# Recommendation tower on one core: loop over pairs of tiles, 14 tables selected on chip in place of 10, MLP on 256 columns

## What is computed

```python
e = jnp.stack([tbl_0[ids[:, 0]], ..., tbl_31[ids[:, 31]]], axis=1)   # 2048 x 32 x 128
dots = jnp.einsum('bfd,bgd->bfg', e, e)
z = dots[:, iu, ju]                                                 # the 496 pairs f < g
h = jnp.concatenate([z, dense_ctx], axis=1)                         # 2048 x 512
h = jnp.maximum(h @ W_top1 + b_top1, 0.0)                           # 512
h = jnp.maximum(h @ W_top2 + b_top2, 0.0)                           # 256
y = h @ W_top3                                                      # 1
```

## Time and profile before

| | |
|---|---|
| median of three runs | 483.03 us (482.62, 486.81, 483.03) |
| span of the profiled execution, first to last instruction | 482.2 us |
| mean granted TensorE clock | 0.915 of full |
| PE busy | 391.0 us, 81% |
| POOL busy | 335.4 us, 70% |
| DVE busy | 240.1 us, 50% |
| ACT busy | 150.2 us, 31% |
| busy share of the 16 DMA engines for gathers (q0), for SP's queue (q1) | 19.4%, 13.9% |
| moved | 41.81 MB |

### The profile page before, as it was taken

One profiled execution on the slowest core, in us unless ns is written; L12 is line 12 of the kernel. 1 busy time (PEld: TensorE's weight loads), 2 busy tenths in 40 slices (PEclk: granted clock), 3 DMA queues, 4 the chain that ended last, 5 costly groups with the idle time before them and its releaser, 6 DMA issues.

```text
span 482.2 us, 16007 instructions
## 1 busy us (share of the span) xinstructions
PE 391.0 (81%) x6624; PEld 362.7 (75%) x6624; DVE 240.1 (50%) x698; ACT 150.2 (31%) x315; POOL 335.4 (70%) x356
## 2 busy tenths in 40 slices
PE   0555669899989898968969898969879798967846
PEld 0554569797979797957969797959879697956836
DVE  1467479556555555635535655535645555411010
ACT  1032223242424243322404332413414232321411
POOL 5777707777777777777777777777777777777700
PEclk9857559899999999989979999989979999988988
DMA  6555843333333323233323333333323332222200
GB/s 139 157 170 175 222 118 89 90 74 91 79 89 76 91 72 90 74 81 79 81 70 83 80 82 86 76 89 77 77 67 87 75 89 63 56 57 53 56 9 0
DMA packets 30470, 41.81 MB, mean 87 GB/s; under 512 B 11986, under 2 KB 23010, under 8 KB 30404
## 3 DMA queue, kind: packets, MB, share of 16 engines
q0 software_dynamic: 11264, 23.09, 19.4%
q1 hardware_dynamic: 16804, 17.52, 13.9%
q10 hardware_dynamic: 2336, 0.19, 0.4%
HBM read 40.76 MB, written 0.01 MB: 85 GB/s over the span
## 4 chain that ended last, share of the span: by engine, by line
PE 59%; issue 12%; DMA 11%; POOL 9%; DVE 6%; ACT 2%; SPq 1%; POOLq 0%; DVEq 0%; ACTq 0%
PE sel_ps L279 26%; DMA rows_T<-tables_selected 11%; PE x_ps L311 10%; PE gram_ps L293 10%; POOL gathered L240 9%; PE rows_ps L264 6%; PE x_ps L320 5%; DVE onehot L500 3%; DVE pairs L508 2%; PE x_ps L327 1%; PE x_ps L302 1%; ACT table_hi L453 1%; DVE pairs L513 1%; DMA gathered<-table,tile_ids 1%; SPq L193 0%
## 5 line engine op out<-in xcount | busy, mean ns | idle before, releaser
L240 POOL DMA_INDIRECT gathered<-table,tile_ids x352 | 335.2, 952 | 122.2 <-issue 103.9
L500 DVE TENSOR_SCALAR onehot<-id_rows,row_no 128x256 fp32r<-128x256 int32 x640 | 198.8, 379 | 94.3 <-PE sel_ps L279 92.7
L279 PE MATMUL sel_ps<-onehot,table_hi 125*128 125x256 f32 x640 | 182.6, 317 | 38.2 <-DVE onehot L500 35.6
L279 PE MATMUL sel_ps<-onehot,table_lo 125*128 125x256 f32 x640 | 173.5, 302 | 2.1 <-issue 2.0
L279 PEld LDWEIGHTS sel_ps<-onehot,table_hi 125*128 125x128 f32 x640 | 134.8, 211 | 47.1 <-issue 43.1
L279 PEld LDWEIGHTS sel_ps<-onehot,table_lo 125*128 125x128 f32 x640 | 135.5, 212 | 0.6 <-issue 0.5
L399 ACT ACTIVATE rows_T<-sel_ps 128x256 f32<-128x256 f32 x80 | 50.4, 630 | 124.3 <-PE sel_ps L279 86.6
L293 PE MATMUL gram_ps<-rows_T 128*32 128x32 f32 x4096 | 57.7, 202 | 35.1 <-issue 31.6
L293 PEld LDWEIGHTS gram_ps<-rows_T 128*32 128x32 f32 x4096 | 47.8, 111 | 45.6 <-issue 41.0
L393 ACT ACTIVATE rows_T<-rows_ps 128x512 f32<-128x512 f32 x96 | 55.9, 589 | 68.8 <-PE rows_ps L264 64.9
L508 DVE STREAM_TRANSPOSE pairs<-gram_ps 128x1024 f32<-128x1024 f32 x16 | 20.0, 1250 | 97.5 <-PE gram_ps L293 97.5
(11 more groups left out here) (12 smaller groups left out, 47.4 us busy)
## 6 DMA issues: line engine op xcount, KB each, us to landing
id_rows<-ids_selected SPq DMA_DIRECT2D x80, 128.0 KB
gathered<-table,tile_ids POOLq DMA_INDIRECT x352
rows_T<-tables_selected SPq DMA_DIRECT2D x10, 500.0 KB
w_sb<-w SPq DMA_DIRECT2D x1, 1024.0 KB, 12.4
w_sb<-w SPq DMA_DIRECT2D x1, 512.0 KB, 14.1
tile_ids<-ids ACTq DMA_DIRECT2D x16, 11.0 KB
out<-y_sb ACTq DMA_DIRECT2D x16, 0.5 KB
mask<-upper_mask SPq DMA_DIRECT2D x1, 128.0 KB, 6.5
```

The source lines that it names most:

```text
L240: nc.gpsimd.indirect_dma_start(gathered[:, a % 2, g, :], None, tables_gathered[g], bass.IndirectOffsetOnAxis(ap=slot_id, axis=0)).then_inc ...
L279: last = nc.tensor.matmul(sel_ps[:, q % 2, 0, :], part[0:SEL_P, f, k, :], onehot[0:SEL_P, h, kk, :], start=(k == 0 and part is table_hi), ...
L500: last = nc.vector.tensor_scalar(onehot[:, h, kk, :], id_rows[:, slot, :], row_no[:, k:k + 1], None, ALU.is_equal)
```

## The change

- 14 tables are selected, 18 features gathered (chunks of 4, 4, 4, 4, 2 per tile, ten chunks in a pair).
- The unit of all loops is a pair of tiles. On PE, `selects(i, o)` holds 13 selections, the turns of chunks 0 to 7 and the network of the pair before; `grams(i, o)` holds the turns of chunks 8 and 9, the two `gram`, and between them the first selection of the next pair. PE, ACT and DVE loop over six pairs with one pair in the body, SP over seven. POOL's program is written out without a loop.
- `layer1`, `layer2`, `layer3` work on the 256 columns of a pair, except in the last pair, which goes through the network tile by tile behind its two `gram`.
- `rows_T` holds two tiles in place of four; a pair's first selection is copied into it after both `gram` of the pair before.
- Tables are loaded into four slots that lie in `pairs`, `x0` and `x1`, each as two transfers, of 112 and of 13 rows. Mask, dense values and weights come behind the last table. Eight of the first pair's ten chunks are turned between the selections of the start.
- All rows of `tile_ids` are loaded at the start, the first tile's by itself.

```diff
-N_SEL = 10
+N_SEL = 14
 SEL_ROWS = 1000
 SEL_K = 8
 SEL_P = SEL_ROWS // SEL_K
+SEL_P16 = SEL_P // 16 * 16
 K_HALF = SEL_K // 2
 N_GATH = N_FEAT - N_SEL
 CHUNK = 4
 CHUNKS = [(c, min(CHUNK, N_GATH - c)) for c in range(0, N_GATH, CHUNK)]
 NC = len(CHUNKS)
-SEL_PER_TILE = N_SEL // 2
 PAIR = 2 * P
-ROW_SLOTS = 4
-RAW_SLOTS = 8
+ROW_SLOTS = 5
+RAW_SLOTS = 4
...
-        rows_T = sb("rows_T", [P, 4, P, N_FEAT])
+        rows_T = sb("rows_T", [P, 2, P, N_FEAT])
...
+        raw_slots = [pairs[:, 0, :, :].rearrange("p g f -> p (g f)"),
+                     pairs[:, 1, :, :].rearrange("p g f -> p (g f)"),
+                     x0[:, :, :].rearrange("p k s -> p (k s)"),
+                     x1[:, :, :].rearrange("p k s -> p (k s)")]
...
+            def load_table(f):
+                if f >= RAW_SLOTS:
+                    sp.wait_ge(table_ready, f - RAW_SLOTS + 1)
+                sp.dma_start(raw(f)[0:SEL_P16, :], tables_selected[f, 0:SEL_P16, :]).then_inc(table_in[f], 16)
+                sp.dma_start(raw(f)[SEL_P16:SEL_P, :], tables_selected[f, SEL_P16:SEL_P, :]
+                             ).then_inc(table_in[f], 16)
+            load_table(0)
             sp.dma_start(row_no[:, :], row_numbers).then_inc(row_no_in, 16)
-            sp.dma_start(raw(0), tables_selected[0]).then_inc(table_in[0], 16)
             load_id_row(0, 0, 0)
+            load_table(1)
...
+            for p in range(n_pairs):
+                for t in range(2):
+                    if p == 0 and t == 0:
+                        pool.wait_ge(first_ids_in, 16)
+                    elif p == 0:
+                        pool.wait_ge(tile_ids_in, 16)
+                    for c, (first, n) in enumerate(CHUNKS):
+                        if p > 0:
+                            pool.wait_ge(chunk_turned, 2 * NC * (p - 1) + NC * t + c + 1)
+                        pool.nop(nofuse=True)
+                        for g in range(first, first + n):
+                            slot_id = tile_ids[:, 2 * p + t, g:g + 1]
+                            nc.gpsimd.indirect_dma_start(
+                                gathered[:, t, g, :], None, tables_gathered[g],
+                                bass.IndirectOffsetOnAxis(ap=slot_id, axis=0)).then_inc(chunk_in[t][c], 16)
...
+            def layer1(i, o, n):
+                if n == 0:
+                    pe.wait_ge(x0_ready, at(i, o, 2, 2))
+                for k in range(K1):
+                    last_op = nc.tensor.matmul(mlp_ps[:, n // 2, n % 2, :], w1_sb[:, k, n * P:(n + 1) * P],
+                                               x0[:, k, :], start=(k == 0), stop=(k == K1 - 1))
+                if n % 2 == 1:
+                    last_op.then_inc(x1_done, 1)
...
+            def selects(i, o):
+                turn_pairs(i, o - 1, 0)
+                turn(i, o, 0)
+                select(i, o, 1)
+                turn_pairs(i, o - 1, 1)
+                select(i, o, 2)
+                turn(i, o, 1)
+                select(i, o, 3)
+                turn(i, o, 2)
...
+                    layer1(i, o - 1, n)
+                    select(i, o, 4 + n)
+                turn(i, o, 3)
+                turn(i, o, 4)
+                select(i, o, 8)
+                layer2(i, o - 1, 0)
+                select(i, o, 9)
+                layer2(i, o - 1, 1)
+                select(i, o, 10)
+                turn(i, o, 5)
+                turn(i, o, 6)
+                select(i, o, 11)
+                layer3(i, o - 1)
+                turn(i, o, 7)
+                for f in range(12, N_SEL):
+                    select(i, o, f)
+                pe.wait_ge(y_ready, at(i, o - 1, 1, 1))
+            def grams(i, o):
+                turn(i, o, 8)
+                gram(i, o, 0)
+                turn(i, o, 9)
+                select(i, o + 1, 0)
+                gram(i, o, 1)
...
-            with pe.Fori(0, n_loops) as i:
-                for a in range(2, 6):
-                    step(i, a)
...
+            with pe.Fori(0, n_pairs - 2) as i:
+                selects(i, 1)
+                grams(i, 1)
+            selects(0, last)
...
+            gram(0, last, 0)
+            turn(0, last, 8)
+            turn_pairs(0, last, 0)
+            turn(0, last, 9)
+            gram(0, last, 1)
+            layer1_tile(0)
+            turn_pairs(0, last, 1)
+            layer2_tile(0)
+            layer1_tile(1)
+            layer3_tile(0)
+            layer2_tile(1)
+            layer3_tile(1)
...
+            def step(i, o):
+                for f in range(2, N_SEL):
+                    compare(i, o, f)
+                compare(i, o + 1, 0)
+                pack_pairs(i, o, 0)
+                compare(i, o + 1, 1)
+                pack_pairs(i, o, 1)
```

More of the change, by code:

```diff
@@ new lines, in turn, with select @@
+                last_op.then_inc(chunk_turned, 1)
+            def select(i, o, f):
+                for h in range(2):
+                    pe.wait_ge(onehot_ready, at(i, o, 2 * N_SEL, 2 * f + h + 1))
+                    if h == 0 and f >= 2:
+                        pe.wait_ge(sel_moved, at(i, o, N_SEL, f - 1))
+                    elif h == 0 and not known_first(i, o):
+                        before = max(g for g in range(N_SEL) if g % 2 == f % 2)
+                        pe.wait_ge(sel_moved, at(i, o - 1, N_SEL, before + 1))
@@ L290, in gram @@
+                    last_op.then_inc(onehot_used, 1)
+            def gram(i, o, t):
+                pe.wait_ge(chunk_moved, at(i, o, 2 * NC, NC * (t + 1)))
+                pe.wait_ge(sel_moved, at(i, o, N_SEL, N_SEL))
+                if not (known_first(i, o) and t == 0):
+                    pe.wait_ge(gram_read, at(i, o, 2, t))
                 for s in range(P // 4):
                     for j in range(4):
-                        rows = rows_T[:, a % 4, j * (P // 4) + s, :]
-                        last = nc.tensor.matmul(gram_ps[32 * j:32 * j + 32, s, :], rows, rows,
-                                                start=True, stop=True)
@@ L295, in gram, with turn_pairs @@
-                last.then_inc(gram_done, 1)
-            def turn_pairs(i, a):
-                pe.wait_ge(pairs_ready, count(i, a, 1, 1))
-                wait_count(pe, x1_ready, count(i, a))
+                        rows = rows_T[:, t, j * (P // 4) + s, :]
+                        last_op = nc.tensor.matmul(gram_ps[32 * j:32 * j + 32, s, :], rows, rows,
+                                                   start=True, stop=True)
+                last_op.then_inc(gram_done, 1)
+            def turn_pairs(i, o, t):
+                pe.wait_ge(pairs_ready, at(i, o, 2, t + 1))
@@ L331, in step @@
-            def step(i, a, rest=True):
-                parts = ([gram], [turn_pairs], [layer1], [layer2], [layer3])
-                for n in range(len(parts)):
-                    turn_chunk(i, a, n)
-                    select(i, *selection(i, a, n))
-                    if rest:
-                        for part in parts[n]:
-                            part(i, a - 1)
-                for c in range(len(parts), NC):
-                    turn_chunk(i, a, c)
+                    last_op = nc.tensor.transpose(
+                        turned_ps(t)[:, k, :],
+                        pairs[:, t, g:g + P // N_FEAT, :].rearrange("p g f -> p (g f)"), ident[:, :])
@@ L363, in _ @@
[L363 to L379 removed]
+                if f == 2:
+                    pe.wait_ge(ident_in, 16)
@@ new lines, in _, with layer1_tile @@
+                if 2 <= f < 10:
+                    turn(0, 0, f - 2)
+            grams(0, 0)
+            pe.wait_ge(weights_in, 80)
+            with pe.Fori(0, n_pairs - 2) as i:
+                selects(i, 1)
+                grams(i, 1)
+            selects(0, last)
+            def layer1_tile(t):
+                pe.wait_ge(x0_ready, 2 * last + t + 1)
+                for n in range(K2):
+                    for k in range(K1):
+                        last_op = nc.tensor.matmul(turned_ps(t)[:, n, :], w1_sb[:, k, n * P:(n + 1) * P],
+                                                   x0[:, k, t * P:(t + 1) * P],
+                                                   start=(k == 0), stop=(k == K1 - 1))
+                last_op.then_inc(x1_done, 1)
@@ L546 @@
+            for f in range(2, N_SEL):
+                compare(0, last, f)
+            pack_pairs(0, last, 0)
+            pack_pairs(0, last, 1)
 def kernel(**inputs):
```

483 lines of the change are left out of this document (230 added, 253 removed).

## The result

The changed kernel takes 514.17 us (median of 4 runs, 509.85 to 519.42) against 482.99 for the kernel before (482.62 to 486.81), a ratio of 1.058 with a 95% interval of 1.050 to 1.065: slower. The forecast was 526 in a range of 490 to 548. The profiled execution took 509.85 us, with a span of 508.0.

What follows compares the result with a forecast made beforehand. PE, almost level with POOL before, was to bound the changed kernel: start 64, first grams 14, six rounds 372, last selections 44 and end 31 give 525 us, 526 with 0.8 outside the span; range 490 to 548.

Steps and rivals of the forecast that it cites:

- Start: Before PE's first gram: 14 split table loads at 3.9 us each and the last selection, 64 us in all.
- That the split does nothing: Rival for the table loads at the start: tables stay 5.1 us apart, 17 us more, 543 in all; 12%.
- Selections: PE's selections in a pair: 14 by 2.00 us make 28.0, which is 8.0 more than before.
- Network on 256 columns: PE's network for a pair: time goes by moving columns, so half as many matmuls still take 11.8 us.
- The rival of fewer instructions: Rival on PE's network: a 256-column matmul costs what one of 128 does; pair 56.1 us, whole 485; 7%.
- Handovers of the one-hot halves: Rival: PE's selections in a row wait for DVE, 2.52 against 2.00 us; 577 if all 14, 544 if five; 14%.
- POOL: POOL's gathers: 36 by 1.25 make 45 us a pair, below PE's 62, so POOL waits and leaves the chain's end.
- End: From the last pair's first gram to the finish, with a second gram and second layer 1 included: 31 us.
- A round: PE's loop over one pair of tiles: 62.0 us against 52.3 before, six rounds making 372.
- one jump back a pair: PE's loop jump, once a pair in place of a half: 3.7 us a pair.
- 2.0 of idle for each: PE's idle time within each of a pair's two grams, waiting for its program: 4.0 us a pair, range 1.9 to 7.6.
- PE's pauses vanish: Rival: the loop's shorter body is held on chip, idle in grams, jumps and rest goes; pair 52.1 us, whole 457; 5%.

Runs made afterwards that it cites:

- the moved kernel: The changed kernel (14 tables) with 39 small unused matmuls ahead of PE's loop, so its body touches seven packets, not eight; ratio 0.948 to the kernel before.
- the slow group: Four kernels (14, 12 and 13 tables moved, 13 unmoved) run with the kernel before, all some 40% slower; kernel before 685.45 us, 486.96 in the previous group.

## Why the prediction was right, and where not

The direction, the size and most terms held; one term came near in its sum, by luck, and was wrong in what it is.

- **Start.** Forecast 64 us to the first gram by two transfers a table, at DVE's pace; measured 66.06. In it PE waits for gathers six times, 8.2 us together, which I had left out ("PE's free time there"); the 2 us may be that. That the split does nothing (12%) would have given 81, and the kernel without it showed 85.44.
- **Selections.** Taken as 2.00 us, measured 1.91 (a layer-1 block, a selection and the next block start at 88.94, 90.67 and 92.58 in the chain of waits). Fourteen are 26.7, not 28.0. The step from 10 to 14 is the largest part of the longer round (7.6 of 7.4, with -0.8 for turns), as forecast.
- **Network on 256 columns.** Forecast no gain, 11.8 us; measured 1.73 for a block of layer 1, 11.3 for the network (six such blocks and layer 3), and the run on 128 columns shows nearly the same time for the same work. Layer 3's row was the right one to go by. The rival of fewer instructions (7%) fell.
- **Handovers of the one-hot halves.** Rival with 14%: 544. PE waits for DVE's compares 4.4 us in the whole run, 11 times. It fell.
- **POOL.** Forecast: over 10 us a pair of waits for PE, and out of the chain's end. 75.3 us over the run, 10.8 a pair, and the chain's end is PE's. That POOL comes level again at 50 us a pair only the kernels with 12 and 11 tables showed; the prediction's 1.25 us a gather gave their pace.
- **End.** Forecast 31, measured 508.0 - 477.31 = 30.7.
- **A round.** Forecast 62.0, measured 59.7, just under the 60 to 64 to which I had given 60%, and over the low end of 56.8. The last round, from which I had taken 4 us for the jump, took 53.3 and not 58: it lost the pauses in its grams too. These two, 14 and 5 us, less the 2 us of the start, make the 17 by which the sum of 525 exceeds the span of 508.0.
- **The step that failed** is "one jump back a pair" beside "2.0 of idle for each" gram. I took both as charged in every round, 4.0 + 3.7, since the earlier trace rows seemed to show "the program being fetched all along". They are one cost, and it is charged only where the body is fetched anew, nine packets at a time: 4.90 at the jump and 0.54 + 3.25 + 1.69 in the grams behind it, then a jump of 0.17 and a body without any fetch. My sign, one pause at the first transposes of every pair and two to four in its grams, did not come: a pair has the one or the other. That 7.7 in every round came near the 6.4 measured is luck. The rows of before couldn't separate this, since its body of 13.3 packets (my count) never stays.
- **The rival "PE's pauses vanish"**, given 5%, named the right mechanism, which the change missed by 0.27 of a packet. I set it aside because "a body of one pair is still several such packets"; several is not yet too many. Its time of 457 would not have come, though. Even a body that is kept has to be fetched once, and the first two rounds pay for it, as with 12 tables. With 53.3 in place of the four rounds from 184.47 to 424.01 (239.5 us) the span would be 508.0 - 26.3 = 482 by my estimate, level with the kernel before; no run at ordinary speed shows it. The ratio of 0.948 of the moved kernel is lower than this, and the slow group doesn't tell why.

The rule of the Trainium skill that the prediction weighed (Runtime: NRT & Kernel Launch, section "Instruction fetch mechanics") says that a taken branch outside a window of two blocks stalls for its target. By that rule each jump of the changed kernel pays. The trace disagrees, with 0.17 and 4.90 in turn, and with 0.21 at the jumps of 12 tables. The same section gives PE's instruction memory as 128 KiB, eight of its blocks; that every body in seven blocks was kept, and none that touches eight was kept in all rounds, agrees with such a size if one block is always the next to be filled. That "if" is my inference; the packets fetched are what is shown.

## What to carry to other kernels

Before a feature is moved from one engine to another, both engines' time for a round has to be worked out: here, without pauses, a pair takes PE 53.3 us and POOL 45 (an estimate by 1.25 us a gather) with 14 tables, and both 50 with 12, which beat 14. Where PE shows idle time put down to "issue" in dense small matmuls or behind a jump, count the packets of its instruction queue and how many the loop's body touches: if it is one too many, shortening the body or moving it by some 150 instructions can be worth nearly as much as the edit itself: by my estimate 26 of 508 us here, where the edit cost 31. A gain at the start reaches the end only in part where another engine sets the middle, as the split showed with 12.1 of 21.4 us.

## What the runs showed of the hardware

- PE keeps a loop's body that lies in seven packets of 16 KB (19 to 21 packets fetched in all, none while the loop repeats, jumps of 0.2 us), and refetches one that touches an eighth, at all five, two or one of its jumps (65 or 66, 38, 29 packets), each time with nine packets. No run here tested a body of six or fewer, nor the other engines.
- What fetching costs depends on where it falls: nothing is seen in selections and layers (packets at 211.1 and 226.1 us, no pause of PE there), 0.5 to 4.0 us at a packet's end inside a gram of the changed kernel (up to 7.8 in the first rounds of 12 tables), 4.4 to 5.1 at a jump. That it is PE's speed through its program which decides is my reading, not tested.
- After such a pause the granted clock is for a while at the lower level (1.2 instead of 2.4 GHz): the four transposes take 1.11 us where they take 0.65 without it, and a selection takes 3.69 us (132.16 to 135.85, granted clock 0.50) where it takes 2.08 (188.44 to 190.52, granted clock 1.00). The granted clock of the round from 123.23 was 0.94, that of the last one 1.00. The pause of 3.98 us thus cost about 1.6 us more than its length in the selection behind it.
- With one transfer of 125 rows of 4 KB a table, tables came 5.3 us apart (14 splits from 7.93 to 77.30); as 112 and 13 rows they came 3.3 to 3.8 apart while ACT still waited for them (12.23 to 26.19). No trace shows which DMA engines took part. This agrees with the Trainium skill (DMA: Bandwidth & Descriptors, section "Why a DMA increments its semaphore by 16 and not by 1"), by which the engines used are the largest number up to 16 that divides the first dimension.
